# Routed expert pairs: products turned two iterations behind gate and up, down four behind, one PSUM bank for the turned products

## The chip, the cores and the metric

One Trainium2 chip, one of its cores. The metric is the device time of one execution in microseconds (us), measured without the profiler, median of several executions. Lower is better.

## What is computed

An AdaLN block over 2 x 1024 tokens of 256 channels, all in fp32: layer norm with a modulation, causal attention with one head of 256, a residual, a second modulated layer norm, and a feed-forward part of one shared expert and 16 routed ones, of which each token uses four:

```python
probs = softmax(xt @ w_router);  top_w, top_i = top_k(probs, 4);  top_w /= sum(top_w)
g = silu(einsum('td,edh->teh', xt, we1)) * einsum('td,edh->teh', xt, we3)   # 16 experts, h = 128
g = g * cw[:, :, None]                        # cw: the weights of the chosen four, else 0
moe_out = einsum('teh,ehd->td', g, we2)
shared = silu(xt @ ws1) * (xt @ ws3) @ ws2    # h = 512
out = shared / 5 + moe_out * 4 / 5
```

## The kernel before

**Stages.** Attention and norms run first (to about 160 us of the profile), then the shared expert in 16 units of 512 tokens (12 of them ahead of the routed part, 4 behind it), then the routed experts. Before the routed part each token's row is scattered by GpSimd to the region of each of its four experts in device memory (`xg`). The regions are cut into tiles of 128 rows; at most 79 of them hold rows. They are worked off in **40 pairs** (`NPAIR`), the last pair with one tile. A pair is loaded from `xg` by SyncE, into a ring of four pairs (`xs`, `RING`) or, for the last six, into places of its own. Its result is scattered by GpSimd to `y_rows` in device memory (`yb`), one indirect DMA for each tile. When all rows that a block of 512 tokens needs have come back, SyncE loads them (`y_in`, 16 loads of 512 KB) and VectorE adds them up.

**Precision.** A product of fp32 values is made of three matmuls on fp32r halves: `split3` at L1816 (hi x hi), L1817 (hi x lo) and L1818 (lo x hi). So each operand needs a rounded part (`_hi`, a copy by ScalarE) and a rest (`_lo`, a subtraction by VectorE).

**The eleven steps of a pair n**, each with its engine and line, and the semaphore that its end raises:

1. `rows_back` (TensorE L2191): four transposes of the loaded rows into bank 6 + n % 2.
2. `x_hi` (ScalarE L1071), then 3. `x_lo_rows` (VectorE L1752, after two small `keep_ends`, L1744).
4. `rows_gate_up` (TensorE, 12 matmuls L1816 to L1818): gate and up of both tiles into bank n % 2.
5. `silu_rows` (ScalarE L1083) reads the gate half.
6. `g_rows` (VectorE L1768, then two products L1771): silu x weight x up, into `r_g`.
7. `g_back` (TensorE L2217): two transposes of the products into bank 2 + n % 2.
8. `g_rows_hi` (ScalarE L1077), then 9. `g_rows_lo` (VectorE L1759).
10. `rows_down` (TensorE, 6 matmuls L1816 to L1818) into bank 4 + n % 2; waits for `gT_lo` of n and for the copy of pair n - 2.
11. `y_rows` (ScalarE L1092), then two scatters (GpSimd L817).

**The order.** Each engine works off its own list, in the order in which its loop (n = 0 to 41) is written, and a wait holds everything behind it. TensorE (L2239 to L2253): `gate_up(n)`, `rows_back(n + 2)`, `g_back(n - 1)`, `down(n - 2)`. ScalarE: `silu(n)`, `x_hi(n + 2)`, `g_hi(n - 1)`, `y(n - 2)`. VectorE: `g_rows(n)`, `x_lo(n + 2)`, `g_lo(n - 1)`; in iterations 37, 38 and 39 an addition of 128 x 1024 (`add_place`, L1497) stands ahead of these. Behind the loop TensorE makes the unit `gate_up(UNITS_FIRST)` of the shared expert between `down(38)` and `down(39)`, and VectorE adds up the places and finishes the blocks.

Of the kernel before, what the change touches and what calls it, by code (L numbers as in the profile page):

```python
# [14 lines left out]
P = 128  # L15
# [220 lines left out]
def adaln_block(nc, x, qkv, o_proj, gamma, beta, w_router, we1, we3, we2, ws1, ws3, ws2, c_in, wmod, out):  # L236
# [3 lines left out]
    with ctx:  # L240
# [154 lines left out]
        tv = sb("tv", [P, 10])  # L395
        spare = sb("spare", [P, NTL])
        places = sb("places", [1, 2 * NTL + NTL], I32)
        assert ORIGIN + 4 * free[0] <= nc.sbuf_usable_end, (ORIGIN + 4 * free[0], nc.sbuf_usable_end)

        def r_part(at_, n):  # L400
# [422 lines left out]
        def _(act):  # L823
# [250 lines left out]
            def g_rows_hi(n):  # L1074

                act.wait_ge(s_rgT, n + 1)
                nc.scalar.activation(gT_hi[:, n % 2].rearrange("p i t -> p (i t)"), ps[:, 2 + n % 2, 0:2 * P],  # L1077
                                     ACT.Copy).then_inc(s_rghi, 1)

            def silu_rows(n):  # L1080

                act.wait_ge(s_rgu, n + 1)
                nc.scalar.activation(r_silu[:, n % 2], ps[:, n % 2, :].rearrange("p (i w) -> p i w", i=2)[:, :, 0:H],  # L1083
                                     ACT.Silu).then_inc(s_rsilu, 1)
# [10 lines left out]
            x_hi(0)  # L1095
            for n in range(NPAIR + 2):
                if n < NPAIR:
                    silu_rows(n)
                if n == 0:
                    x_hi(1)  # L1100
                if n + 2 < NPAIR:
                    x_hi(n + 2)
                if 0 <= n - 1 < NPAIR:
                    g_rows_hi(n - 1)
                if n == NPAIR + 1:
                    silu_step(UNITS_FIRST)
                if 0 <= n - 2:
                    y_rows(n - 2)

# [5 lines left out]
        def _(dve):  # L1115
# [640 lines left out]
            def g_rows_lo(n):  # L1756

                dve.wait_ge(s_rghi, n + 1)
                nc.vector.tensor_tensor(gT_lo[:, n % 2].rearrange("p i t -> p (i t)"), ps[:, 2 + n % 2, 0:2 * P],  # L1759
                                        gT_hi[:, n % 2].rearrange("p i t -> p (i t)").bitcast(F32), ALU.subtract  # L1760
                                        ).then_inc(s_rglo, 1)

            def g_rows(n):

                dve.wait_ge(s_rsilu, n + 1)
                dve.wait_ge(s_kept, kept(n))
                of = slice(2 * n, 2 * n + len(tiles_of(n)))
                nc.vector.tensor_tensor(dest[:, of], ends[:, n, 0:len(tiles_of(n)), 0].bitcast(I32),  # L1768
                                        aside[:, 0, of], ALU.max).then_inc(s_rg, 1)
                for i in tiles_of(n):  # L1770
                    nc.vector.scalar_tensor_tensor(out=r_g[:, n % 2, i, :], in0=r_silu[:, n % 2, i, :],  # L1771
                                                   scalar=ends[:, n, i, 1:2],
                                                   in1=ps[:, n % 2, i * D + H:(i + 1) * D], op0=ALU.mult,
                                                   op1=ALU.mult).then_inc(s_rg, 1)

            x_lo_rows(0)
            shared_out(UNITS_FIRST // SH - 1)
            for n in range(NPAIR + 1):
                if n in ADDED_AHEAD:
# [5 lines left out]
                if n + 2 < NPAIR:  # L1785
                    x_lo_rows(n + 2)
                if 0 <= n - 1:
                    g_rows_lo(n - 1)
            add_place(NB - 1, 2)
# [23 lines left out]
        def _(pe):  # L1813
# [381 lines left out]
            def rows_gate_up(n, of):  # L2195

                pe.wait_ge(s_rxlo, n + 1)
                if n < 2:
                    pe.wait_ge(s_g, UNITS_FIRST - 1)
                if n == 0:  # L2200
                    pe.wait_ge(s_whi_r, E)
                    pe.wait_ge(s_wlo_r, E)
                for i in tiles_of(n):
                    for c in range(DC):
                        last = split3(ps[:, n % 2, i * D:(i + 1) * D],
                                      (xT_hi[:, n % 2, i, c, :], xT_lo[:, n % 2, i, c, :]),
# [4 lines left out]
            def g_back(n):  # L2211

                pe.wait_ge(s_rg, products(n))
                if n < 2:
                    pe.wait_ge(s_g, UNITS_FIRST)
                for i in tiles_of(n):
                    last = nc.tensor.transpose(ps[:, 2 + n % 2, i * P:(i + 1) * P], r_g[:, n % 2, i, :], ident[:])  # L2217
                last.then_inc(s_rgT, 1)
# [20 lines left out]
            for n in range(NPAIR + 2):  # L2239
                done_pairs = n - 2  # L2240
                if done_pairs > 0 and done_pairs % 8 == 0 and HELD + done_pairs <= NPAIR:
                    load_experts(HELD + done_pairs - 8, HELD + done_pairs, done_pairs - 8)
                if n < NPAIR:
                    of[n] = experts_of(n)
                    rows_gate_up(n, of[n])
                if n + 2 < NPAIR:
                    rows_back(n + 2)
                if 0 <= n - 1 < NPAIR:
                    g_back(n - 1)
                if n == NPAIR + 1:  # L2250
                    gate_up(UNITS_FIRST)
                if 0 <= n - 2:
                    rows_down(n - 2, of[n - 2])  # L2253

# [39 lines left out]
```

## Time and profile before

| | us |
|---|---|
| median of 3 runs, not profiled | 339.36 (338.07 to 340.48) |
| span of the profiled execution | 380.7 |
| difference of the two | 41.3 |

The span is that of one execution under the hardware profiler, from its first to its last instruction; no other time of that execution is given, so what lies around the span isn't known. It is 12% longer than the median of the executions without the profiler. Starts, durations and waits below are those of the profiled execution. The end of a matmul in the profile is modelled, not observed, and matmuls overlap: their pitch from start to start tells more than their duration.

### The profile page before, as it was taken

To read this page: it belongs to the slowest core of one execution; us is meant where nothing else is said; L and a number is where in the kernel's file an instruction comes from. 1 tells how busy PE (TensorE), PEld (TensorE's weight loads), DVE (VectorE), ACT (ScalarE), POOL (GpSimd) and SP (SyncE) were. 2 spreads that over 40 slices of the span, in tenths; PEclk is the share of its full clock that TensorE was granted. 3 is DMA by queue.
4 is the path that set the end of the run, shared out by engine and by line. 5 is a ranking of instruction groups with operands and counts; after the bars stand their busy time and mean duration, and the time that the engine had idled before them with its cause. 6 is when DMAs were issued, how large, how long until landed. Compare 5 with 4: busy or idle time off the path is not lost.

```text
span 380.7 us, 7758 instructions
## 1 busy us (share of the span) xinstructions
PE 333.3 (88%) x2252; PEld 297.6 (78%) x2252; DVE 255.2 (67%) x806; ACT 190.3 (50%) x440; POOL 200.8 (53%) x285
## 2 busy tenths in 40 slices
PE   8989999999999999868889897788778877887995
PEld 5778898888899898736778796777667767877784
DVE  1889998999887756219986744543454345448797
ACT  2667777767865665414234444443444355346300
POOL 2687754357867655746740064555455545545820
PEclk9999999999999999969999999999999999999999
DMA  8236600002213996322232466556445544788824
GB/s 271 75 104 205 209 17 27 16 31 87 85 65 118 316 312 214 119 85 78 104 117 76 121 209 183 155 171 194 149 124 171 164 133 136 264 302 327 261 86 165
DMA packets 42280, 57.55 MB, mean 151 GB/s; under 512 B 5144, under 2 KB 34592, under 8 KB 42240
## 3 DMA queue, kind: packets, MB, share of 16 engines
q1 hardware_dynamic: 34288, 35.42, 30.7%
q0 software_dynamic: 6864, 19.80, 13.5%
q10 hardware_dynamic: 1088, 1.84, 1.5%
q8 instruction: 20, 0.33, 0.4%
q14 instruction: 20, 0.16, 0.2%
HBM read 32.64 MB, written 24.40 MB: 150 GB/s over the span
## 4 chain that ended last, share of the span: by engine, by line
PE 43%; DVE 27%; issue 13%; another core or an unknown queue 7%; ACT 7%; DMA 1%; POOL 1%; DVEq 0%; ACTq 0%
PE ps L1816 10%; PE ps L1818 10%; PE ps L1817 9%; PE ps L1990 4%; DVE y_in L1497 3%; DVE r_g L1771 2%; DVE gT_lo L1759 2%; ACT r_silu L1083 2%; DVE negmax L1626 2%; PE ps L2191 2%; PE ps L2092 1%; PE ps L1823 1%; DMA wmod_sb<-in_L_wmod_dram 1%; DVE bn L1197 1%
## 5 line engine op out<-in xcount | busy, mean ns | idle before, releaser
L817 POOL DMA_INDIRECT y_rows<-y_sb,aside x72 | 70.5, 980 | 87.9 <-ACT y_sb L1092 71.7
L776 POOL DMA_INDIRECT xg_rows<-hrow,slot_u x64 | 65.6, 1024 | 27.8 <-issue 20.0
L1816 PE MATMUL ps<-rpool 128*128 128x256 f32 (+3 forms) x152 | 49.8, 328 | 2.7 <-DVE rpool L1221 1.1
L1768 DVE TENSOR_TENSOR aside<-ends,aside 128x2 int32<-128x2 int32 (+1 forms) x40 | 6.3, 157 | 62.9 <-ACT r_silu L1083 55.4
L1816 PE MATMUL ps<-w_hi_routed,xT_hi 128*128 x158 | 45.2, 286 | 1.8 <-DVE xT_lo L1752 1.8
L1083 ACT ACTIVATE r_silu<-ps 128x256 f32<-128x256 f32 x40 | 15.8, 395 | 61.4 <-PE ps L1818 51.4
L1818 PE MATMUL ps<-rpool 128*128 128x256 f32 (+3 forms) x152 | 46.0, 302 | 0.0
L1817 PE MATMUL ps<-rpool 128*128 128x256 f32 (+3 forms) x152 | 45.9, 302 | 0.0
L1818 PE MATMUL ps<-w_hi_routed,xT_lo 128*128 x158 | 44.7, 283 | 0.0
L1817 PE MATMUL ps<-w_lo_routed,xT_hi 128*128 x158 | 44.6, 283 | 0.0
L1816 PE MATMUL ps<-w_hi_routed,gT_hi 128*128 x79 | 25.8, 326 | 15.1 <-DVE gT_lo L1759 15.0
L1816 PEld LDWEIGHTS ps<-rpool 128*128 128x128 f32 x152 | 28.8, 190 | 6.0 <-DVE rpool L1221 2.5
L1816 PEld LDWEIGHTS ps<-w_hi_routed,xT_hi 128*128 128x128 f32 x158 | 30.2, 191 | 2.5 <-issue 2.3
L1752 DVE TENSOR_TENSOR xT_lo<-ps,xT_hi 128x512 fp32r<-128x512 f32 x40 | 27.4, 684 | 6.2 <-ACT xT_hi L1071 6.0
L1817 PEld LDWEIGHTS ps<-w_lo_routed,xT_hi 128*128 128x128 f32 x158 | 30.2, 191 | 0.0
L1818 PEld LDWEIGHTS ps<-w_hi_routed,xT_lo 128*128 128x128 f32 x158 | 30.2, 191 | 0.0
L1816 PEld LDWEIGHTS ps<-w_hi_routed,gT_hi 128*128 128x128 f32 x79 | 14.9, 188 | 19.5 <-issue 19.4
L1818 PEld LDWEIGHTS ps<-rpool 128*128 128x128 f32 x152 | 28.8, 189 | 1.1
L1817 PEld LDWEIGHTS ps<-rpool 128*128 128x128 f32 x152 | 28.9, 190 | 0.9
L1816 PE MATMUL ps<-h2T_hi,w_hi_shared 128*128 128x512 f32 x64 | 27.3, 426 | 1.4 <-issue 0.9
L1071 ACT ACTIVATE xT_hi<-ps 128x512 fp32r<-128x512 f32 x40 | 24.4, 612 | 8.0 <-remote 5.8
L1817 PE MATMUL ps<-h2T_lo,w_hi_shared 128*128 128x512 f32 x64 | 25.6, 400 | 2.6 <-issue 2.6
(236 smaller groups left out, 928.8 us busy)
## 6 DMA issues: line engine op xcount, KB each, us to landing
xs<-xg_rows SPq DMA_DIRECT2D x68, 144.0 KB
y_in<-y_rows SPq DMA_DIRECT2D x16, 512.0 KB
xg_rows<-empty SPq DMA_DIRECT2D x4, 576.0 KB, 3.8
x_in<-in_L_attn_x_dram SPq DMA_DIRECT2D x16, 128.0 KB, 2.1
w_raw_routed<-in_L_ffn_we_dram SPq DMA_DIRECT2D x8, 256.0 KB
out_dram<-x SPq DMA_DIRECT2D x14, 128.0 KB, 1.8
xs_own<-xg_rows SPq DMA_DIRECT2D x11, 144.0 KB
wmod_sb<-in_L_wmod_dram ACTq DMA_DIRECT2D x3, 512.0 KB, 6.6
```

Of the source, the lines that this page charges most:

```text
L776: nc.gpsimd.indirect_dma_start(out=xg, out_offset=bass.IndirectOffsetOnAxis(ap=slot_u[:, t, k:k + 1].bitcast(U32), axis=0), in_=hrow[:, t, ...
L817: nc.gpsimd.indirect_dma_start(out=yb, out_offset=bass.IndirectOffsetOnAxis(ap=dest[:, 2 * n + i:2 * n + i + 1].bitcast(U32), axis=0), in_ ...
L1071: nc.scalar.activation(xT_hi[:, n % 2].rearrange("p i c t -> p (i c t)"), ps[:, 6 + n % 2, :], ACT.Copy).then_inc(s_rxhi, 1)
L1083: nc.scalar.activation(r_silu[:, n % 2], ps[:, n % 2, :].rearrange("p (i w) -> p i w", i=2)[:, :, 0:H], ACT.Silu).then_inc(s_rsilu, 1)
L1497: then(nc.vector.tensor_tensor(y[0], y[0], y[k], ALU.add))
L1626: nc.vector.tensor_reduce(negmax[:, t % 4:t % 4 + 1], score_banks(t), AX.X, ALU.max, negate=True).then_inc(tl["negmax"], 1)
L1752: nc.vector.tensor_tensor(xT_lo[:, n % 2].rearrange("p i c t -> p (i c t)"), ps[:, 6 + n % 2, :], xT_hi[:, n % 2].rearrange("p i c t -> p ...
L1759: nc.vector.tensor_tensor(gT_lo[:, n % 2].rearrange("p i t -> p (i t)"), ps[:, 2 + n % 2, 0:2 * P], gT_hi[:, n % 2].rearrange("p i t -> p ...
L1816: nc.tensor.matmul(dst, w[0], x_[0], start=first, stop=False)
L1817: nc.tensor.matmul(dst, w[0], x_[1], start=False, stop=False)
L1818: return nc.tensor.matmul(dst, w[1], x_[0], start=False, stop=last)
L1990: last = nc.tensor.matmul(to, unit(n)[1][:, tok], w_raw_s[:, e, W2:WX], start=(e == 0 and b < NB - 1 and j % 2 == 0), stop=(e == SH - 1), ...
```

## The change

TensorE's loop becomes `down(n - 4)`, `gate_up(n)`, `rows_back(n + 2)`, `g_back(n - 2)`, ScalarE's `y(n - 4)`, `silu(n)`, `x_hi(n + 2)`, `g_hi(n - 2)`, and VectorE's `g_rows(n)`, `x_lo(n + 2)`, `g_lo(n - 2)`. Gate and up rotate through banks 0, 1 and 2 instead of 0 and 1, the SiLU and the products through three buffers instead of two. The turned products go to bank 3 alone instead of banks 2 and 3, so `g_back(n)` also waits until `g_lo(n - 1)` has read it. The two buffers of `gT_hi` and `gT_lo` and the banks of `down` stay. Behind the loop, `down(38)`, the shared unit and `down(39)` follow in the order they had.

```diff
+        g_third = sb("r_g_third", [P, 2, H])
+        silu_ring = (r_silu[:, 0], r_silu[:, 1], at("r_silu_third", HR + RING * 2 * (ROW + D), [P, 2, H])[:])
+        g_ring = (r_g[:, 0], r_g[:, 1], g_third[:])
+        def gT_of():
+            return ps[:, 3, 0:2 * P]
@@ ScalarE: g_rows_hi, silu_rows
-                nc.scalar.activation(gT_hi[:, n % 2].rearrange("p i t -> p (i t)"), ps[:, 2 + n % 2, 0:2 * P],
-                                     ACT.Copy).then_inc(s_rghi, 1)
+                nc.scalar.activation(gT_hi[:, n % 2].rearrange("p i t -> p (i t)"), gT_of(), ACT.Copy
+                                     ).then_inc(s_rghi, 1)
-                nc.scalar.activation(r_silu[:, n % 2], ps[:, n % 2, :].rearrange("p (i w) -> p i w", i=2)[:, :, 0:H],
+                nc.scalar.activation(silu_ring[n % 3], ps[:, n % 3, :].rearrange("p (i w) -> p i w", i=2)[:, :, 0:H],
@@ ScalarE: the loop
             for n in range(NPAIR + 2):
+                if 0 <= n - 4:
+                    y_rows(n - 4)
                 if n < NPAIR:
                     silu_rows(n)
...
-                if 0 <= n - 1 < NPAIR:
-                    g_rows_hi(n - 1)
-                if n == NPAIR + 1:
-                    silu_step(UNITS_FIRST)
                 if 0 <= n - 2:
-                    y_rows(n - 2)
+                    g_rows_hi(n - 2)
+            y_rows(NPAIR - 2)
+            silu_step(UNITS_FIRST)
+            y_rows(NPAIR - 1)
@@ VectorE: g_rows and the loop
-                    nc.vector.scalar_tensor_tensor(out=r_g[:, n % 2, i, :], in0=r_silu[:, n % 2, i, :],
+                    nc.vector.scalar_tensor_tensor(out=g_ring[n % 3][:, i, :], in0=silu_ring[n % 3][:, i, :],
                                                    scalar=ends[:, n, i, 1:2],
-                                                   in1=ps[:, n % 2, i * D + H:(i + 1) * D], op0=ALU.mult,
+                                                   in1=ps[:, n % 3, i * D + H:(i + 1) * D], op0=ALU.mult,
-            for n in range(NPAIR + 1):
+            for n in range(NPAIR + 2):
...
-                if 0 <= n - 1:
-                    g_rows_lo(n - 1)
+                if 0 <= n - 2:
+                    g_rows_lo(n - 2)
@@ TensorE: rows_gate_up, g_back
-                if n < 2:
-                    pe.wait_ge(s_g, UNITS_FIRST - 1)
+                if n < 3:
+                    pe.wait_ge(s_g, UNITS_FIRST - (n < 2))
...
-                        last = split3(ps[:, n % 2, i * D:(i + 1) * D],
+                        last = split3(ps[:, n % 3, i * D:(i + 1) * D],
...
                 pe.wait_ge(s_rg, products(n))
-                if n < 2:
-                    pe.wait_ge(s_g, UNITS_FIRST)
+                if n > 0:
+                    pe.wait_ge(s_rglo, n)
                 for i in tiles_of(n):
-                    last = nc.tensor.transpose(ps[:, 2 + n % 2, i * P:(i + 1) * P], r_g[:, n % 2, i, :], ident[:])
+                    last = nc.tensor.transpose(gT_of()[:, i * P:(i + 1) * P], g_ring[n % 3][:, i, :], ident[:])
@@ TensorE: the loop
-                done_pairs = n - 2
+                done_pairs = n - 4
...
+                if 0 <= n - 4:
+                    rows_down(n - 4, of[n - 4])
                 if n < NPAIR:
                     of[n] = experts_of(n)
                     rows_gate_up(n, of[n])
                 if n + 2 < NPAIR:
                     rows_back(n + 2)
-                if 0 <= n - 1 < NPAIR:
-                    g_back(n - 1)
-                if n == NPAIR + 1:
-                    gate_up(UNITS_FIRST)
                 if 0 <= n - 2:
-                    rows_down(n - 2, of[n - 2])
+                    g_back(n - 2)
+            rows_down(NPAIR - 2, of[NPAIR - 2])
+            gate_up(UNITS_FIRST)
+            rows_down(NPAIR - 1, of[NPAIR - 1])
```

## Rows read from the trace of the kernel before

**Rows 1.** The page's head: the span, and each engine's busy time.
```profile
span 380.7 us, 7758 instructions
PE 333.3 (88%) x2252; PEld 297.6 (78%) x2252; DVE 255.2 (67%) x806; ACT 190.3 (50%) x440; POOL 200.8 (53%) x285
```

**Rows 2.** Busy time by stage (windows): two stretches of the loop, and the tail.
```profile
core 0: us, PE busy (x) PEld busy (x) DVE busy (x) ACT busy (x) POOL busy (x), PEclk, DMA share, GB/s
214.00:228.60 14.60, 14.60 (x125) 14.47 (x125) 6.99 (x28) 6.75 (x15) 5.77 (x6) 1.00 0.65 197
228.60:350.00 121.40, 97.01 (x767) 90.05 (x766) 59.03 (x232) 54.67 (x132) 61.83 (x64) 1.00 0.60 193
...
354.50:381.00 26.50, 21.88 (x101) 18.32 (x99) 21.76 (x24) 3.48 (x6) 7.53 (x7) 0.97 0.49 164
```

**Rows 3.** Waits from 209 to 352 us: waiter, releaser: us in total, times, longest.
```profile
ACT r_silu L1083 <- PE ps L1818: 51.4, 18, 4.1
...
PE ps L1816 <- DVE gT_lo L1759: 15.0, 17, 1.5
...
PE ps L2217 <- DVE r_g L1771: 9.2, 12, 0.9
```

**Rows 4.** Timeline, pairs 3 and 4, no wait: start, us, engine, line, tiles, count.
```profile
218.36 0.28 PE L1816 MATMUL ps<-w_hi_routed,xT_hi 128*128 x1
...
219.80 0.60 PE L2191 MATMUL ps<-ident,xs 128*128 128x128 f32 x4
220.00 0.39 ACT L1083 ACTIVATE r_silu<-ps 128x256 f32<-128x256 f32 x1 [0.84 <-PE ps L1818]
...
220.38 0.36 PE L1816 MATMUL ps<-w_hi_routed,gT_hi 128*128 x1
...
220.50 0.60 DVE L1771 SCALAR_TENSOR_TENSOR r_g<-r_silu,ends,ps 128x128 f32<-128x128 f32 x2
...
220.93 0.38 ACT L1077 ACTIVATE gT_hi<-ps 128x256 fp32r<-128x256 f32 x1
...
221.17 0.28 PE L1816 MATMUL ps<-w_hi_routed,xT_hi 128*128 x1
...
221.76 0.41 DVE L1759 TENSOR_TENSOR gT_lo<-ps,gT_hi 128x256 fp32r<-128x256 f32 x1
...
223.04 0.38 PE L2217 MATMUL ps<-ident,r_g 128*128 128x128 f32 x2
...
223.18 0.36 PE L1816 MATMUL ps<-w_hi_routed,gT_hi 128*128 x1
```

**Rows 5.** Timeline, one cycle of two pairs with its waits, in brackets.
```profile
248.57 0.29 PE L1818 MATMUL ps<-w_hi_routed,xT_lo 128*128 x1
...
251.74 0.38 ACT L1083 ACTIVATE r_silu<-ps 128x256 f32<-128x256 f32 x1 [3.69 <-PE ps L1818]
...
252.89 0.44 PE L2217 MATMUL ps<-ident,r_g 128*128 128x128 f32 x2 [0.79 <-DVE r_g L1771]
...
253.49 0.41 DVE L1759 TENSOR_TENSOR gT_lo<-ps,gT_hi 128x256 fp32r<-128x256 f32 x1
...
254.05 0.38 PE L1816 MATMUL ps<-w_hi_routed,gT_hi 128*128 x1 [0.72 <-DVE gT_lo L1759]
```

**Rows 6.** GpSimd's scatters of the loop (lines): busy, mean ns, idle before, releasers.
```profile
L817 POOL DMA_INDIRECT y_rows<-y_sb,aside x72 | 70.5, 980 | 87.9 <-ACT y_sb L1092 71.7 <-issue 16.2
```

**Rows 7.** Timeline: second group of `y_in` loads, first addition that needs them.
```profile
331.10 10.01 SPq L672 DMA_DIRECT2D y_in<-y_rows  x6
...
345.53 1.21 DVE L1497 TENSOR_TENSOR y_in<-y_in,y_in 128x1024 f32<-128x1024 f32 x1
```

**Rows 8.** Timeline of the loop's end: last of gate and up, then the shared unit.
```profile
351.31 0.28 PE L1818 MATMUL ps<-w_hi_routed,xT_lo 128*128 x1
...
354.52 0.39 PE L1816 MATMUL ps<-h2T_hi,w_hi_shared 128*128 128x512 f32 x1
...
358.10 0.69 DVE L1461 SCALAR_TENSOR_TENSOR act_kept<-act_kept,ps 128x512 f32<-128x512 f32 x1 [1.34 <-issue]
```

More of the change, by code:

```diff
@@ L1758, in g_rows_lo @@
                 dve.wait_ge(s_rghi, n + 1)
-                nc.vector.tensor_tensor(gT_lo[:, n % 2].rearrange("p i t -> p (i t)"), ps[:, 2 + n % 2, 0:2 * P],
+                nc.vector.tensor_tensor(gT_lo[:, n % 2].rearrange("p i t -> p (i t)"), gT_of(),
                                         gT_hi[:, n % 2].rearrange("p i t -> p (i t)").bitcast(F32), ALU.subtract
```

## The prediction, written before the changed kernel had run

> **What bounds the kernel now.** I read the page's head first: TensorE is busy 88% of the span, VectorE 67%, GpSimd 53%, ScalarE 50% [rows 1]. The diff touches only the routed loop, so the next view is the busy time by stage. It shows two different loops. From 214 to 228.6 us TensorE has no gap: 125 matmuls in 14.6 us, 8.56 in a us. From 228.6 to 350 it starts 767 in 121.4 us, 6.32 in a us [rows 2]. A pair has 12 + 4 + 2 + 6 = 24 matmuls and transposes, so a pair costs 2.80 us in the first stretch and 3.80 in the second. At the first stretch's rate the 767 would have taken 89.6 us; 31.8 us are lost. The waits say how: TensorE stood 15.0 us in 17 waits for `gT_lo` and 9.2 us in 12 for the products, and ScalarE stood 51.4 us in 18 waits for gate and up [rows 3]. The timeline shows why. A gate and up ends by its record at 248.57 + 0.29 = 248.86, but the SiLU that it releases starts at 251.74, after 3.69 us of an idle ScalarE [rows 5]. In the first stretch the same step took nothing: gate and up runs from 218.36 to about 219.96, the SiLU starts at 220.00 [rows 4]. So in the second stretch the news that a gate and up is done reaches ScalarE 2.88 us late, every second pair, and all that TensorE waits for afterwards hangs on that.
>
> Is this lateness there without the profiler? The execution without it is 41.3 us shorter, and the loop's 31.8 us are the largest loss in the trace that could go. No other stage offers so much: the engines' busy times can't go, and the clock is 1.00 in these windows [rows 2]. I take it that most of the lateness belongs to the profiled execution, and that the loop runs near its gapless 2.80 us a pair otherwise: 31.8 of 41.3 us. That is an inference, and a rival below drops it.
>
> **The change part by part.**
>
> *Work removed or added: none.* All 24 matmuls, 4 ScalarE and 7 VectorE operations of a pair, its scatters and its loads stay, with their shapes. A third buffer or bank costs no time. TensorE's sum for 40 pairs stays 40 x 2.80 = 112 us. A loop bound by TensorE's own work can't gain from a change of order.
>
> *Where the slack is now.* In the gapless stretch, count from the end of gate and up of pair 3 at 219.96. The products are ready at 221.10 (220.50 + 0.60) and `g_back(3)` starts at 223.04: 1.94 us to spare. `g_lo(2)` ends at 221.76 + 0.41 = 222.17 and `down(2)`, which needs it, starts at 223.18: 1.01 us to spare [rows 4]. The thinner one, `gT_lo`, decides.
>
> *Products turned two behind.* `g_back(n)` moves later by one iteration, 2.80 us or more. Its wait for the products gets 1.94 + 2.80 = 4.74 us of slack, so even a SiLU that is 2.88 us late is hidden: the 9.2 us of [rows 3] go from this place.
>
> *Down four behind.* It moves from the end of iteration n + 2 to the head of n + 4, past one iteration's other work, and its own wait for `gT_lo` becomes slack of 2 us and more: the 15.0 us of [rows 3] go from this place too.
>
> *The one bank for turned products.* Here is what is late next. `g_back(n - 2)` now waits for `g_lo(n - 3)`. VectorE does `g_lo(n - 3)` at the end of its iteration n - 1, at the same place behind `g_rows` and `x_lo` as before. That is 222.17 - 219.96 = 2.21 us after gate and up of n - 1 ends. TensorE reaches `g_back(n - 2)` one iteration of 2.80 us and one `rows_back` (220.24 would be its end: 4 x 0.11 = 0.44) after the same moment: 3.24 us. The slack is 1.03 us, as much as before [rows 4]. Behind the waiting `g_back` stand `down`, the next gate and up and all else of TensorE. So the loop gets back the old slack at a new place.
>
> *The held cycle redone.* From 248.86: before, TensorE works to 252.10 (252.89 less its 0.79 idle), waits for the products, turns them, waits again, and starts `down` at 254.05, 5.19 us after the start of the count [rows 5]. After the change it does `rows_back`, `g_back`, `down`, gate and up, `rows_back`, the same matmuls, to about the same 252.10, and then waits for the `gT_lo` that VectorE ends at 253.49 + 0.41 = 253.90 [rows 5]. It resumes at 254.05 too. But the two transposes (0.22 us), which before lay within the wait, now lie behind it. With 17 such cycles [rows 3] that is 17 x 0.14 to 0.22 = 2.4 to 3.7 us more, if every hold is as long as before. If there is no hold, it is nothing.
>
> *First iterations.* `gate_up(2)` must wait for the shared unit 11's product, which VectorE finished before the loop; nothing. TensorE has less to do in iterations 1 to 3 and exactly that more behind the loop; nothing.
>
> *ScalarE's head.* `y(n - 4)` stands ahead of `silu(n)` now. Its `down` ended one gate and up (1.4 us) earlier and it takes 0.60, so it is over in time. Bound from the other side: if GpSimd lets the ring of four results run full, the wait stands before a SiLU in either order; same price.
>
> *GpSimd.* A scatter has 0.98 us and 0.30 of issue, 2.53 us a pair [rows 6], under 2.80. The results come one iteration later at first, and more tightly at the end, where GpSimd ends some 2.5 us later. It had ended well before the last additions; hidden. Cover gone, it costs those 2.5.
>
> *Loads of `y_in`.* They come with the scatters, one iteration (2.8 to 3.8 us) later. Before, the second group was issued at 331.10 and first needed at 345.53, 14.4 us on. A load of 512 KB at the 193 GB/s of [rows 2] takes 2.7 us. 11.7 us of slack cover the shift [rows 2, 7].
>
> *The end of the loop.* Behind it VectorE is busy 21.76 of 26.5 us [rows 2], and what starts its first wait of 1.34 us is the shared unit on TensorE, which starts at 354.52, 2.93 us behind the last gate and up (351.59) [rows 8]. These 2.93 us hold 3 transposes and 12 matmuls, 3 x 0.11 + 12 x 0.12 = 1.77, and 1.16 of waits. Afterwards the last gate and up comes 0.94 us earlier (one `down` and one `g_back` less ahead of it). Behind it stand 5 transposes and 18 matmuls, 2.71 us. The waits on the one bank add to that. A turn is 0.28 + 0.42 + 0.45 = 1.15 us against 0.94 of work, some 0.2 to 0.3 for the last, and 0.5 for the first, behind the last SiLU. 2.71 + 0.8 - 0.94 = 2.57: 0.4 us earlier. All of VectorE's chain behind it is unchanged.
>
> **Sum.** In the profiled execution: 380.7 + (2.4 to 3.7) - 0.4 = 382.7 to 384.0. Without holds: -0.4. The median of the runs shown is 339.36; I expect it between 339.0 and, with the holds at the scale of 339.4 to 380.7, 341.9. I take 340.0, nearer to the case without holds.
>
> The Trainium skill, Perfetto Trace Analysis, Optimizing Tensor Performance, says that independent groups of matmuls should rotate through several PSUM banks, so that reading one bank overlaps the next group. Gate and up follow it further than before, but the turned products now go against it, and that is the second rival. The same page, Identifying Performance Opportunities, says that a gap that repeats on the engine that should be full can mean too few buffers; by that the third bank and buffers should close the gaps, which is the first rival.
>
> **Rivals.**
>
> *1. It does what it says: the waits of 15.0 and 9.2 us are real and go.* For it: they repeat 17 and 12 times at the two steps that the change moves [rows 3]. Against: the one bank's wait has the same releaser, and the 41.3 us say that not much of it can be there without the profiler. All 24.2 us gone would be 339.4 - 24.2 = 315.2. What can be left without the profiler is at most what isn't in the 41.3; if a third of the waits is real, 339.4 - 8 = 331. Chance 0.20, at 325 to 336.
>
> *2. The one bank becomes the limit, and it is slower.* The place is `g_back(n - 2)` behind `g_lo(n - 3)`. It decides once `gT_lo` is over 1.03 us late in every pair, or the iteration is shorter than the 2.80 us of the profile. Each 0.1 us of wait a pair costs 4 us. For it: the wait is new, and slack is no larger than before. Against: [rows 4] has 1 us left. 0.1 to 0.2 us a pair gives 343.4 to 347. Chance 0.17.
>
> *3. Late loads.* `y_in` late by more than its slack would stall VectorE in iterations 37 to 39 and with it the loop. 11.7 us against 3.8 [rows 7]; chance 0.03, at 343 to 346.
>
> *4. My forecast, no change that shows:* 0.60.
>
> **How the numbers follow.** A change of about 1% is what a measurement of this kernel can tell from none. Faster by over 1% is rival 1 with a little from tight sums: 0.22. Slower by over 1% is rivals 2 and 3, less their mild halves: 0.18. Within 1%: 0.60. The range goes from 331, the upper part of rival 1, to 345, the middle of rival 2; about 0.1 is left out below and 0.06 above. The forecast's own range is 337.5 to 342.
>
> **What would show it.** Right: the waits of L2217 for `r_g` and of the down matmuls for `gT_lo` are gone, and L2217 waits for `gT_lo` L1759 instead, about 17 times, some 1.8 us each. A pair costs 3.8 us in the profile of after too, and 2.80 where no SiLU is held. Wrong, to the fast side: TensorE's matmuls from 228 to 350 come at more than 7 in a us, with few waits of L2217. Wrong, to the slow side: waits of L2217 in every pair, or VectorE's L1497 idle for a load. The median would be wrong with the profile right if the holds are real and change their rhythm with the order of the steps; nothing in these rows says what ends a hold.

## The result, and the profile after

The changed kernel took 342.66 us (median of 4 executions, 341.98 to 342.86) beside 339.68 us for the kernel before (4 executions, 338.07 to 340.48). The ratio is 1.0073 with an interval from 1.0052 to 1.0094: slower by 0.7%, some 2.5 to 3 us. That lies within the 1% that was called no change, and within the stated range of 331 to 345, but not where the forecast put its number, 340.0 (0.3 us above the 339.68 of the kernel before), and 0.7 us beyond the forecast's own range of 337.5 to 342.

The profile of the changed kernel looks nothing like [rows 1]: the profiled execution is as fast as the others. The page's head, with the span and each engine's busy time:

```profile
span 340.2 us, 7796 instructions
PE 324.0 (95%) x2252; PEld 296.5 (87%) x2252; DVE 255.9 (75%) x806; ACT 196.1 (58%) x440; POOL 202.6 (60%) x285
```

The busy times answer to [rows 1] within 10 us for TensorE and 1 to 6 for the rest. 7,758 instructions have become 7,796, 38 more, and no engine's count of busy ones has changed. They come back below.

The busy time by stage, the loop and then the tail, as in [rows 2]:

```profile
212.40:309.60 97.20, 96.15 (x809) 94.49 (x807) 61.41 (x237) 62.31 (x135) 65.38 (x67) 1.00 0.71 225
313.00:340.20 27.20, 22.89 (x106) 19.22 (x106) 22.19 (x25) 4.17 (x8) 9.44 (x8) 0.98 0.66 236
```

TensorE starts 809 matmuls in 97.2 us, 8.32 in a us: near the 8.56 of the stretch without gaps in [rows 2], not the 6.32 of its other stretch. What is left of TensorE's waits, from the start of the loop to the shared unit behind it (waiter, releaser: us in total, times, longest), where [rows 3] had 15.0 and 9.2 us:

```profile
PE ps L1825 <- DVE xT_lo L1761: 1.9, 2, 1.7
PE ps L1825 <- issue: 0.9, 2, 0.6
PE ps L2226 <- DVE gT_lo L1768: 0.8, 2, 0.6
```

Each line is small. ScalarE's longest wait for a gate and up is 0.9 us, where [rows 3] had 4.1; there is no cycle like [rows 5] anywhere. So the kernel after must be compared with a kernel before in which nothing was held, and that takes a second profile of the kernel before. It is the first experiment.

One measure is used throughout. The loop is counted from the start of the first gate and up to the end of the last, then to the shared unit's first matmul, then to VectorE's step that needs it (3.58 us later in all but one of the kernels), then to the end (22.6 us). A period is the time from one pair's gate and up to the next one's.

### The profile page after: what moved, and what is told of

Same layout as the page of the kernel before. It is cut to its first block, busy times and chain, and to the rows that moved or that the text cites. A ratio compares the mean times of both kernels' runs of the same rounds, so it can differ in the third digit from the quotient of the medians.

```text
span 340.2 us, 7796 instructions
## 1 busy us (share of the span) xinstructions
PE 324.0 (95%) x2252; PEld 296.5 (87%) x2252; DVE 255.9 (75%) x806; ACT 196.1 (58%) x440; POOL 202.6 (60%) x285
## 4 chain that ended last, share of the span: by engine, by line
PE 61%; DVE 21%; issue 9%; ACT 4%; POOL 2%; DMA 1%; DVEq 0%; ACTq 0%; POOLq 0%
PE ps L1825 14%; PE ps L1826 13%; PE ps L1827 13%; PE ps L1999 5%; PE ps L2200 5%; DVE y_in L1506 3%; PE ps L2226 3%; DVE negmax L1635 2%; PE ps L1832 1%; PE ps L2101 1%; DMA wmod_sb<-in_L_wmod_dram 1%; PE ps L1934 1%; DVE bn L1206 1%; DVE y_in L1516 1%; DVE rpool L1628 1%
## 5 line engine op out<-in xcount | busy, mean ns | idle before, releaser
L784 POOL DMA_INDIRECT xg_rows<-hrow,slot_u x64 | 66.5, 1038 | 22.4 <-issue 20.0
L1827 PE MATMUL ps<-h2T_hi,w_lo_shared 128*128 128x512 f32 x64 | 25.1, 392 | 0.0
L1091 ACT ACTIVATE r_silu<-ps 128x256 f32<-128x256 f32 x27 | 10.4, 383 | 25.2 <-PE ps L1827 23.5
```

The costliest lines, as they stand in the source:

```text
L784: nc.gpsimd.indirect_dma_start(out=xg, out_offset=bass.IndirectOffsetOnAxis(ap=slot_u[:, t, k:k + 1].bitcast(U32), axis=0), in_=hrow[:, t, ...
L1091: nc.scalar.activation(silu_ring[n % 3], ps[:, n % 3, :].rearrange("p (i w) -> p i w", i=2)[:, :, 0:H], ACT.Silu).then_inc(s_rsilu, 1)
L1827: return nc.tensor.matmul(dst, w[1], x_[0], start=False, stop=last)
```

## The experiments

**The kernel before, profiled again.**

> The kernel before, unchanged, profiled again. Theory A (the late news of the first profile belongs to that one execution, since the kernel after had a profiled span of 340.2 us against 342.7 without the profiler): the span comes out near 338 us, the routed loop runs at 2.80 to 2.85 us a pair with no cycle of two pairs, and ScalarE waits for gate and up well under 51 us. Theory B (the profiler slows this order of the steps and not the other): span near 381 us again, 17 long waits of the SiLU. Without the profiler 339.4 us either way.

Measured: 340.1 us, ratio 1.0005 (0.9981 to 1.0029), profiled span 338.6 us. Its busy time by stage, the loop from about pair 4 on:

```profile
212.40:309.80 97.40, 97.32 (x825) 96.52 (x823) 62.95 (x243) 63.66 (x138) 66.35 (x68) 1.00 0.74 234
```

And all of TensorE's waits from the start of the loop to the shared unit:

```profile
PE ps L1816 <- DVE xT_lo L1752: 1.7, 1, 1.7
PE ps L2217 <- DVE r_g L1771: 0.4, 1, 0.4
```

The waits of 15.0 and 9.2 us of [rows 3] are not there, in the same kernel. They belonged to that one execution. TensorE is busy 97.32 of 97.40 us, with 8.47 matmuls in a us, so this stretch of the kernel before was full, and no order of the steps could make it faster by more than its small gaps, 1.1 us in all. The kernel after lost about 1 us of this: 96.15 of 97.20.

The periods read from the two traces (computed from the starts of the gate and ups) say where. All are 2.80 or 2.81 us, pair 3 to pair 36, but for these:

```
us above 2.81, of the period that starts at pair
                  3     7     9    10    11    15    17    18    19    23    31   sum
before, again     -    .15   .06   .10    -    .34   .12   .10    -    .17   .09   1.1
after            .17   .28    -     -    .90   .32    -     -    .55   .28   .32   2.8
```

The largest two, 0.90 and 0.55, stand at pairs 11 and 19. At the end of these iterations TensorE's sequencer loads the numbers of the next eight pairs' experts (`load_experts`, a register load of L2156). They are 1.45 of the 1.7 us by which the two sums differ.

**Two banks, the change's order.** The changed kernel with gate and up in banks 0 and 1, and turned products in banks 2 and 3. The wait for `g_lo(n - 1)` goes; gate and up of pair n has to wait for the products of n - 2 in its place.

```diff
-            return ps[:, 3, 0:2 * P]
+            return ps[:, 2 + n % 2, 0:2 * P]
...
-                if n < 3:
-                    pe.wait_ge(s_g, UNITS_FIRST - (n < 2))
+                if n < 2:
+                    pe.wait_ge(s_g, UNITS_FIRST - 1)
+                else:
+                    pe.wait_ge(s_rg, products(n - 2))
...
                 pe.wait_ge(s_rg, products(n))
-                if n > 0:
-                    pe.wait_ge(s_rglo, n)
+                if n < 2:
+                    pe.wait_ge(s_g, UNITS_FIRST)
```

> The kernel after, but gate and up alternate in banks 0 and 1 and the turned products in banks 2 and 3 as before; the order two and four behind and the rings of three stay. Theory 1 (the one bank for turned products makes the 2.9 us): 339 to 340.5 us, ratio to before 0.999 to 1.002. Theory 2 (the deeper order itself makes it, through four instead of three downs and two more turns behind the last gate and up): 342 to 343 us, ratio 1.006 to 1.009, as the kernel after.

Measured: 339.75 us, ratio 0.9993 (0.9975 to 1.0010), span 337.9. The whole loss is gone. The order of the steps costs nothing; the single bank, or its wait, costs all of it. The number of instructions is not what costs either: this kernel has the same 7,796, since here gate and up has a second wait in 38 pairs.

**One bank, the order of before.** The other half alone: the kernel before, with its turned products in bank 3 and the wait that this needs.

```diff
-                if n < 2:
+                if n == 0:
                     pe.wait_ge(s_g, UNITS_FIRST)
+                if n > 0:
+                    pe.wait_ge(s_rglo, n)
```

> The kernel before, but all turned products in bank 3, with the wait for gT_lo of the pair ahead that this needs; order and rings as before. g_back(n) now waits for g_lo(n - 1), which in the old order comes at the end of the same iteration of VectorE, behind x_lo. Theory 1 (the bank costs): 342 us or more, since here the wait has one iteration less of slack: g_lo(n - 1) ends some 2.2 us behind gate and up of n, and TensorE comes to g_back(n) 3.2 us behind it, so still 1.0 to spare in the loop and a loss only at the end, 340 to 342. Theory 2 (the order costs, not the bank): 339 to 340, ratio 0.999 to 1.002.

Measured: 342.03 us, ratio 1.0059 (1.0033 to 1.0084), span 340.9. The loop takes 113.11 us against 111.17 of before: 1.94 us. In the change's order the same step made 111.84 against 109.93: 1.91. The price of the single bank in the loop is the same in both orders, but it is made up differently: the periods that hold the two register loads (pairs 9 and 17 in this order) grew by 0.92 us and not 1.45, and those of pairs 7, 23 and 31 by 1.0.

**The wait alone, two banks.** The kernel of two banks above, with the wait put back though nothing needs it.

```diff
                 pe.wait_ge(s_rg, products(n))
                 if n < 2:
                     pe.wait_ge(s_g, UNITS_FIRST)
+                if n > 0:
+                    pe.wait_ge(s_rglo, n)
```

> Two banks for the turned products as in e1, which needs no such wait, with the wait of the kernel after added all the same: g_back(n) waits for gT_lo of n - 1, written second. If the wait makes the cost, through TensorE's sequencer, and not the shared bank as memory, the time is that of after: 342.2 to 343, ratio 1.006 to 1.009, and the periods of iterations 11 and 19 are 3.4 us or more. If the bank as memory makes it, 339.5 to 340.3, ratio 0.998 to 1.001.

Measured: 343.1 us, ratio 1.0099 (1.0071 to 1.0128), span 341.2; the loop is 112.40 us and what lies between it and the shared unit 4.48. That is all of the loss and 0.56 us more in the loop than in the kernel after; why more wasn't tested (this kernel has the second wait of gate and up besides). Sharing the bank has no part in the loss: it is the wait.

How can a wait cost time that TensorE never stands in? The timeline of the changed kernel, end of iteration 11 (start, us, engine, line, tiles, and in brackets the idle time before):

```profile
228.47 0.28 PE L1825 MATMUL ps<-w_hi_routed,xT_hi 128*128 x1
...
229.06 0.41 DVE L1768 TENSOR_TENSOR gT_lo<-ps,gT_hi 128x256 fp32r<-128x256 f32 x1
...
230.34 0.38 PE L2226 MATMUL ps<-ident,r_g 128*128 128x128 f32 x2
...
231.37 0.38 PE L1825 MATMUL ps<-w_hi_routed,gT_hi 128*128 x1 [0.65 <-issue]
```

`gT_lo`, which the wait is for, is ready at 229.47, and the transposes that need it start at 230.34. They are 0.87 us later, so the wait doesn't hold them. Then `down` comes 1.03 us behind them, and the profile can only say "issue". The same place with two banks, where `down` follows in 0.14 us:

```profile
230.54 0.38 PE L2228 MATMUL ps<-ident,r_g 128*128 128x128 f32 x2
230.68 0.36 PE L1825 MATMUL ps<-w_hi_routed,gT_hi 128*128 x1
```

The records of TensorE's sequencer, which the profile doesn't count as busy, have the rest. Their start and duration, counted in us from the start of the same gate and up (228.47 in the kernel after):

```
                                 after            two banks        two banks and the wait
own wait of g_back, for g_lo     1.04, 0.05       none             1.03, 0.05
load of the expert numbers       1.17, 1.32       0.02, 1.23       1.16, 1.23
next wait (down's, for a bank)   2.54, 0.05       1.31, 0.05       2.44, 0.05
first matmul of down             2.90             2.02             2.65
```

`g_back` has two waits now. One has no record of its own, so it rides on the transpose; the other has become an instruction of its own (`EVENT_SEMAPHORE`, 39 of them, L2224), and the sequencer stands before it until 229.47 + 0.04. The sequencer usually runs ahead of the array: with two banks it is at the register load 0.02 us after the gate and up has started, with 2.0 us of matmuls still queued, and the load's 1.23 us are hidden. With the wait it gets there at 1.17, ends the load at 2.49, and the last transpose has started at 1.98. TensorE has run dry.

**The load taken out of the wait's way.** If this is right, moving the load ahead of `g_back` must bring back 1.45 us.

```diff
-                done_pairs = n - 4
-                if done_pairs > 0 and done_pairs % 8 == 0 and HELD + done_pairs <= NPAIR:
-                    load_experts(HELD + done_pairs - 8, HELD + done_pairs, done_pairs - 8)
+                done_pairs = n - 3
...
                     rows_back(n + 2)
+                if done_pairs > 0 and done_pairs % 8 == 0 and HELD + done_pairs <= NPAIR:
+                    load_experts(HELD + done_pairs - 8, HELD + done_pairs, done_pairs - 8)
```

> The kernel after, with TensorE's two loads of expert numbers within the loop (1.3 us each on the sequencer) moved from the head of iterations 12 and 20 to ahead of g_back in iterations 11 and 19, where the sequencer waits anyway. In after the periods of iterations 11 and 19 are 3.71 and 3.36 us against 2.81. Theory S (held sequencer, load no longer covered): these two come down to 2.8 to 2.9, 1.3 us less, 341.2 to 341.6, ratio 1.003 to 1.006. Theory D: unchanged, 342.5.

Measured: 341.11 us, ratio 1.0031 (1.0013 to 1.0049), span 339.1. The periods at 11 and 19 are 2.80: both gaps are gone. The one at 15 grew from 0.32 to 0.58 above 2.81, so the loop gained 1.18 us and not 1.45.

**The two waits in the other order.** Only the line order of `g_back`'s two waits changes.

```diff
-                pe.wait_ge(s_rg, products(n))
                 if n > 0:
                     pe.wait_ge(s_rglo, n)
+                pe.wait_ge(s_rg, products(n))
```

> The kernel after, with the two waits of g_back written in the other order. In the trace of after the wait for gT_lo, written second, is an instruction of its own on TensorE's sequencer, which holds everything behind it from being prepared; the first wait rides on the transpose itself. Swapped, the wait for the products, which is long fulfilled, is the one that stands alone. Theory S (the one bank costs through the held sequencer: 1.9 us in the loop of 111.8): the loop comes back to 110 us, the time to 340.7 to 341.3, ratio to before 1.001 to 1.004. Theory D (the bank costs by the data's own lateness): unchanged, 342.5, ratio 1.006 to 1.009.

Measured: 341.92 us, ratio 1.0047 (1.0028 to 1.0066), span 338.6: between the two forecasts. Now the sequencer's own instruction is the wait for the products, which is met before it gets there (at -0.11 us on the scale above). But the load still starts at 1.05, so here it waits behind the transpose that carries the other wait, and the gaps at 11 and 19 stay, 0.82 and 0.54. An unmet wait ahead of the load holds the sequencer in either form, as an instruction of its own or on the transpose. What goes is 0.4 us of the small ones at pair 3 and at every eighth pair: their sum over pairs 3, 7, 15, 23 and 31 is 1.37 in the kernel after and 0.97 here. At pairs 7, 15, 23 and 31 the sequencer itself is behind in every kernel (0.1 to 0.3 us a time in the kernel before too): it has no record for 1.9 to 2.2 us there, in the kernel before, after and with two banks. In iteration 15 of the kernel after it comes to the wait at 1.97 us, long after `gT_lo` is ready, and the transpose, `down`'s wait and the rest stand behind one instruction more; with the waits swapped that instruction was done before the pause, at -0.09.

**Both.**

> The kernel after with both edits: the waits of g_back swapped (111.3 us from the first to the last gate and up instead of 111.8) and the loads of expert numbers moved (110.7). If they save separately, 110.2 us, close to the 109.9 with two banks, and 4.2 to 4.4 us behind the last gate and up as in after: 340.6 to 341.2, ratio 1.001 to 1.004. If they save the same, 341.1 to 341.9, ratio 1.003 to 1.006.

Measured: 339.86 us, ratio 1.0002 (0.9985 to 1.0019), span 339.3: below both forecasts. The loop is 110.02 us, against 109.93 with two banks; its end is 4.18 us, and 3.52 with two banks. The two savings add up and the single bank costs no more in the loop: 1.45 us of its 1.91 were the two register loads, the other 0.45 the extra instruction at pair 3 and at every eighth pair.

**VectorE's additions one iteration earlier.** This one goes for the end of the loop. In the changed kernel an addition of a block (L1506, 1.2 us) stands ahead of the last products and turned products on VectorE.

```diff
-ADDED_AHEAD = {NPAIR - 3: NB - 1, NPAIR - 2: 0, NPAIR - 1: 1}
+ADDED_AHEAD = {NPAIR - 4: NB - 1, NPAIR - 3: 0, NPAIR - 2: 1}
```

> The kernel after, with VectorE's three additions ahead of the routed work in iterations 36, 37 and 38 instead of 37, 38 and 39. Behind the last gate and up TensorE takes 4.39 us to the shared unit in after, 3.52 with two banks, 2.70 before. If the addition ahead of the last products is what makes the turns on one bank late, the 4.39 become 3.7 or less and the time 341.8 to 342.2; if the chain of turns alone does, they stay within 0.2. If the loads of y_in are late for iteration 36 (the first landed 2.8 us ahead of its use in after), VectorE stalls there and the time is 342.7 or more.

Measured: 342.81 us, ratio 1.0085 (1.0064 to 1.0106), span 340.6: no gain. The last gate and up stands 4.06 us ahead of the shared unit instead of 4.39, but the loop is 0.24 longer. The additions explain a third of a microsecond of the end at most. The rest is the chain on the single bank:

```profile
311.54 0.41 PE L2226 MATMUL ps<-ident,r_g_third 128*128 128x128 f32 x2 [0.60 <-DVE gT_lo L1768]
...
312.98 0.30 PE L2226 MATMUL ps<-ident,r_g 128*128 128x128 f32 x1 [0.23 <-DVE gT_lo L1768]
...
314.04 0.39 PE L1825 MATMUL ps<-h2T_hi,w_hi_shared 128*128 128x512 f32 x1
```

This is the kernel after, behind its last gate and up, which ends at 309.65 (here the wait is a true wait of the array). `g_back(38)` waits for the `gT_lo` of 37, and `g_back(39)` for that of 38. The second of these turns took 1.44 us from start to start, the first 1.79, with VectorE's addition in it. With two banks the last gate and up ends 3.52 us before the shared unit, with one 4.39: 0.87 us. With two banks and the wait it was 4.48, so here too it is the wait that costs.

**A first attempt at something faster.** In the kernels above TensorE waits 1.65 us ahead of pair 1's gate and up, since ScalarE and VectorE split its rows behind pair 0's SiLU and the shared expert's addition. Here, on top of the two banks, the splits of pair 1 come first, and no longer in iteration 0.

```diff
             x_hi(0)
+            x_hi(1)
...
             x_lo_rows(0)
+            x_lo_rows(1)
             shared_out(UNITS_FIRST // SH - 1)
```

> Two banks for the turned products as in e1, and the rounding of pair 1's rows moved ahead: x_hi(1) before the first SiLU, x_lo(1) before the shared expert's addition on VectorE. In all traces TensorE waits 1.65 to 1.7 us for it between gate and up of pairs 0 and 1. If this wait is on the path, the time falls by 1.5 us or so: 338 to 338.8, ratio 0.993 to 0.997, faster than before and than e1. If the addition of the shared expert, now later, or the first down, which waits for it, takes its place, 339.5 to 340.5.

Measured: 339.35 us, ratio 0.9978 (0.9963 to 0.9993), span 338.3. The wait of 1.65 us is gone, but pair 2's gate and up now waits 1.43 us for the products of pair 0, behind the same addition. Of 1.65 us some 0.3 were won in the loop of this profile.

**The shared addition spread out.** Then the addition, 2.5 us of VectorE, was put behind the products of pairs 0, 1 and 2 and the split that follows each, one piece each.

> e7 with the shared expert's three operations on VectorE (3.7 us in all with their gaps, ahead of the loop until now) spread one each behind x_lo of iterations 0, 1 and 2; down(0), which waits for the first two, comes in iteration 4 only. In e7 the wait of 1.65 us after the first gate and up went and one of 1.43 us after the second took its place, behind those operations. If they were its cause, no wait over 0.5 us is left there and the time is 337.6 to 338.6, ratio 0.992 to 0.996. If the loads of rows from device memory set the pace of the first pairs, 339.3 as e7.

Measured: 343.05 us, ratio 1.0083 (1.0051 to 1.0115), span 341.0. It undid everything, and neither forecast had it. The loop's first three periods were 1.88, 1.86 and 2.09 us, as hoped, and the next ones 3.99, 5.27 and 4.34. SyncE's queue, the last piece of the addition on VectorE and what TensorE waited for:

```profile
205.33 1.22 DVE L1802 TENSOR_TENSOR x<-x,gated 128x1024 f32<-128x1024 f32 x1
...
206.78 0.86 SPq L653 DMA_DIRECT2D xs_own<-xg_rows  x2
...
207.83 5.20 SPq L653 DMA_DIRECT2D xs<-xg_rows  x5
...
211.68 0.66 PE L2217 MATMUL ps<-ident,xs 128*128 128x128 f32 x4 [2.20 <-DMA xs<-xg_rows]
```

A load of rows (`xs_own`), which by the program waits for this addition (`s_shared`), goes out 0.23 us after it ends, 3.56 us later than in the kernel it is built on (203.22), and the loads that follow in the same queue wait behind it. TensorE then stood 2.20 us, and worse came after. The busy time of three stretches, with the granted clock before the last two numbers:

```profile
210.00:212.00 2.00, 0.32 (x3) 0.32 (x4) 0.84 (x5) 0.00 (x0) 0.96 (x1) 1.00 0.81 226
212.00:214.00 2.00, 2.00 (x17) 2.00 (x15) 1.09 (x3) 1.47 (x3) 0.00 (x0) 0.77 0.34 90
214.00:216.00 2.00, 2.00 (x11) 2.00 (x11) 0.03 (x1) 0.09 (x1) 1.48 (x2) 0.50 0.52 139
```

After a stretch with TensorE busy 0.32 of 2 us the granted clock fell to 0.50, the 1.2 GHz level, for the two microseconds from 214 (11 matmuls where 17 had been), and was back at 1.00 from 218 on. A loop without gaps is worth keeping without gaps for this too.

**The shared unit ahead of `down(38)`, and the first attempt again.** The last try at the end of the loop, with the kernel of the first attempt beside it on the same chip.

```diff
-            rows_down(NPAIR - 2, of[NPAIR - 2])
             gate_up(UNITS_FIRST)
+            rows_down(NPAIR - 2, of[NPAIR - 2])
...
-            y_rows(NPAIR - 2)
             silu_step(UNITS_FIRST)
+            y_rows(NPAIR - 2)
```

> The kernel of e7 (two banks for gates, two for turned products, the second split ahead of the first SiLU), and one step more at the end of the loop: the shared unit 12's gate and up stands ahead of the down of pair 38 on TensorE, and its SiLU ahead of that pair's result on ScalarE. Nothing is left out. In e7's trace the unit's first matmul starts 3.52 us behind the last gate and up, 0.72 of it (six matmuls of 0.12) the down of pair 38. Between e7's last loop wait and the end VectorE has no gap from the step at 315.76 on, and its work ahead of that step ends at 315.15. Theory A, VectorE's chain behind the unit sets the end: the step comes 0.6 us earlier (VectorE's additions allow no more), and the span with it, 0.9960 of before against 0.9978 of e7. Theory B, the results of pairs 38 and 39 and with them GpSimd's last scatters come about 1 us later, and the last load of y_in waits for them: then VectorE's additions behind 324 get a wait, and the gain is eaten, 0.998 to 1.001.

> The kernel of e7 once more, to see whether its small gain holds beside e11 on one chip: 0.9978 of before was measured, with an interval from 0.9963 to 0.9993. Theory A, the two banks and the earlier split are a real gain of 0.4 us of order and the 0.3 us that the first iterations showed: 0.997 to 0.999. Theory B, it was the spread of the measurement: 1.000, with an interval that holds 1.

Measured: 338.9 us, ratio 0.9972 (0.9956 to 0.9989), span 337.3, for the former; 338.72 us, ratio 0.9961 (0.9939 to 0.9983), span 337.0, for the latter. The step of VectorE behind the shared unit came 0.7 us earlier, counted from the last gate and up, as the first theory said, and then the time from it to the end was 23.28 us instead of 22.59. Neither theory had named what took it back:

```profile
317.16 0.60 ACT L919 ACTIVATE act_t<-ps 128x512 f32<-128x512 f32 x1 [2.03 <-PE ps L1825]
317.79 0.69 DVE L1469 SCALAR_TENSOR_TENSOR act_t<-act_t,ps 128x512 f32<-128x512 f32 x1 [0.66 <-ACT act_t L919]
```

VectorE has a wait of 0.66 us at the next unit, 13, which it hasn't in the other kernel (there the step starts at 317.49 with no idle time before it). TensorE still had all of `down(38)` to do before that unit. At the end TensorE's sum of work counts, not only what stands ahead of the first unit. The kernel of the first attempt has held its small gain: 0.9978 and 0.9961, both intervals below 1. By 0.2 to 0.4% it is faster than the kernel before, and so than both kernels of the study; the loop of its second profile is 109.29 us, against 109.64.

## Why the prediction was right or wrong

*The late news of gate and up belongs to one execution.* Right, and the most important step: [rows 3] and [rows 5] gave waits of 24 us on TensorE that a change of order seems made for, and rival 1 rested on them. In the second profile of the kernel before they are 0.4 us. The argument was only that 41.3 us of span over the median must sit somewhere; it could have been checked no further without a second trace. What made ScalarE's news late in that execution stays open. It came in one profile of the 14 taken of the kernels here.

*The profiled execution of the changed kernel, 382.7 to 384.0.* It couldn't be tested: there were no holds in it. The sum for the case without holds was -0.4 us. It splits so, by the kernel with two banks, which has the change's order and not its bank:

| us, kernel after less before | predicted | measured |
|---|---|---|
| loop, by the order of the steps | -0.94 | -1.24 |
| loop, by the single bank | 0 | +1.91 |
| end of the loop | +0.58 | +1.69 (order 0.82, bank 0.87) |
| sum | -0.4 | +2.4 |

Loop and end are read from the traces: 111.17 and 2.70 us before, 109.93 and 3.52 with two banks, 111.84 and 4.39 after. By the medians the sum is 3.0. The spans differ by only 1.6, since the part ahead of the loop, which the change doesn't touch, happened to be 0.8 shorter in the profiled execution of the kernel after.

*Products two behind, `down` four behind.* Right that they cost nothing and that a loop full of TensorE's work can't gain from them. *First iterations, "nothing".* Slightly off: the loop's first three periods take 7.75 us instead of 8.76, TensorE having less to do there, and the work that comes back at the end is 0.82.

*The one bank's slack of 1.03 us.* Here is the step that failed. The slack itself was well read from [rows 4]: `gT_lo` was ready 0.87 us before the transposes in iteration 11. The text concluded that "the loop gets back the old slack at a new place" and priced the wait at nothing. It counted what is queued behind the wait on the array: `down`, the next gate and up. It didn't ask what the wait does to TensorE's sequencer, which runs up to 2 us ahead of the array and does more than issue matmuls. An unmet wait takes this lead away. In the kernel after it is an instruction of the sequencer; on the transpose it does the same (with the waits swapped the load starts at 1.05 us). The sequencer, which with two banks passes this place about 1 us before `gT_lo` is ready, had no slack, and at two places, where a register load of 1.2 to 1.3 us comes next, the array ran dry. With the small gaps at pair 3 and every eighth pair that is 1.91 us, beside the 0.87 at the end. `load_experts` at the head of an iteration, between the wait and `down`, wasn't counted.

*Rival 2, the one bank becomes the limit, 343.4 to 347.* Its place was right and its mechanism wrong. It wanted 0.1 to 0.2 us of wait in every pair; 27 of the 34 periods from pair 3 to pair 36 stayed at 2.79 to 2.81. The condition, `gT_lo` more than 1.03 us late in every pair, never came. The single bank's loss comes at seven places.

*The end of the loop, 2.93 us before and 3.5 after.* The work was right (18 matmuls and 5 transposes, 2.71 us), the waits were not: 4.39 - 2.71 = 1.68 us instead of 0.8 (these are the steps of [rows 8]). Even with two banks 3.52 - 2.71 = 0.81 us are waits, so the 0.8 would have been right for a change without the single bank; the chain of three turns on one bank adds 0.87. The prediction put a turn at 1.15 us; the two in the trace took 1.79 and 1.44. The rest of the tail didn't change: from the shared unit on it is 26.2 us in both kernels.

*GpSimd and the loads of `y_in`.* Hidden, as said. The scatters, which answer to [rows 6]:

```profile
L825 POOL DMA_INDIRECT y_rows<-y_sb,aside x72 | 71.0, 986 | 52.5 <-ACT y_sb L1100 40.9 <-issue 11.3 <-DMA y_rows<-y_sb,aside 0.3
```

The second group of loads and its addition, which answer to [rows 7]:

```profile
298.17 11.98 SPq L680 DMA_DIRECT2D y_in<-y_rows  x9
...
304.74 1.22 DVE L1506 TENSOR_TENSOR y_in<-y_in,y_in 128x1024 f32<-128x1024 f32 x1
```

The first load of this group is the one that the addition needs. But it is issued only 6.57 us ahead of its use, not 14.4 less 3.8, because the loop runs its last pairs in 2.8 us and not in 3.8; it landed at 301.9, with 2.8 us to spare. The 11.7 us of slack of the prediction were those of the held execution.

*What would show it.* It named waits of L2217 (now L2226) for `gT_lo` about 17 times as the sign of being right. The changed kernel has 2, both at the end: that sign belonged to the holds. What came is the sign that it gave for being wrong on the fast side, more than 7 matmuls in a us and few waits (8.32 here), with a time that was slower and not faster, since the loop of before had no holds either. So the number came within the stated range with some luck: a median near 340 was forecast for a loop with the old slack, and what came was 1.9 us of a new loss in the loop, 0.9 at its end and 0.4 won by the order. That 0.7% was called no change hides this too: the interval, 1.0052 to 1.0094, tells it from none. Two small slips in the sums change nothing: two scatters of 0.98 and 0.30 us make 2.56 and not 2.53, and the upper end of the holds, 384.0 scaled to the median, is 342.3 and not 341.9.

The Trainium skill, Perfetto Trace Analysis, Optimizing Tensor Performance, has the rule that groups of matmuls should rotate through several banks. The runs agree with it in part (two banks 0.9993, one bank 1.0073, or 1.0059 in the old order; but one bank with the two edits 1.0002), and not by its reason: the transposes never had to wait for the bank to be read out, but in the last two pairs. The same page, Identifying Performance Opportunities, says that repeating gaps, as those of [rows 3], can mean too few buffers; the second trace has the same buffers and no such gaps.

## What to carry to other kernels

Before a wait is called free because its condition is met in time for the array, ask which engine's sequencer executes it, how far that sequencer runs ahead, and what else it does next; a register load that was hidden behind a queue of matmuls comes to light when an unmet wait takes that lead away. Where a profiled execution is 12% longer than the median, take a second profile before its waits are used for anything. And when work is moved to the end of a loop, count the waits of a chain that has nothing beside it any more, there the wait of a single buffer shows first.

## What was not expected of the hardware

- A second wait ahead of a transpose became an instruction of TensorE's sequencer: 38 more instructions in the trace, 0.05 us each by their records. Their number costs nothing (two banks: as many, 0.9993); a wait that isn't met yet when the sequencer comes to it cost 1.9 us in the loop, 1.45 of them at two register loads.
- A register load of eight pairs' numbers from on-chip memory takes 1.11 to 1.52 us on TensorE's sequencer (5 of them, median 1.32; the two in the loop 1.32 and 1.11). It is free with a lead of 2.0 us and costs 0.55 to 0.90 us where the sequencer comes to it 1.15 us later.
- The order of two waits in the program matters: the first rides on the matmul, the second becomes the sequencer's, and swapping them took 0.4 us from the loop's small gaps. It didn't free the register loads.
- Every eighth pair takes 0.1 to 0.3 us more in all kernels, with TensorE's sequencer late: a pause of 1.9 to 2.2 us without a record. What it does there was not found.
- One profiled execution of the kernel before was 42 us longer than the next one of the same kernel, with the news of a gate and up 2.88 us late at ScalarE, every second pair. It wasn't met again.
